# Attention's edge stage: scores spread by adding transposes instead of products with the identity

## The chip, the cores and the metric

The kernel runs on one core of a Trainium2 chip. The metric is the device time of one execution, in microseconds (us). It was run three times before the change: 25516.59, 25548.4 and 25451.02 us, median 25516.59.

## The reference, cut to what matters

Four graph layers follow one another on 6250 nodes and 206250 edges that are sorted by their destination. The change lies in the second, an attention layer. For each edge it makes four scores `a`, takes a softmax of them over the edges that share a destination, and sums weighted messages there:

```
a = (m1_s @ W_alpha).reshape(e, H, AS_)          # H = 4
a = jnp.where(a > 0, a, 0.2 * a)
a = jnp.sum(a * alpha_dot, axis=-1, keepdims=True)
amax = jax.ops.segment_max(a, dst, num_segments=n)
...
ex = jnp.exp(a - amax[dst])
den = jax.ops.segment_sum(ex, dst, num_segments=n)
alpha = ex / (den[dst] + 1e-16)
...
agg = jax.ops.segment_sum(alpha * h, dst, num_segments=n)
```

All values are 32-bit floats.

## The kernel before, in words

The program goes through its stages one after the other, each a block with five engine programs: prepare, sorting the edges (names `order_...`), the first layer's edges, its nodes, the attention layer's edges (`edge_layer1`), its nodes, and then edges and nodes twice more. Only `edge_layer1` is touched.

`edge_layer1` handles 1620 tiles of 128 edges, one edge on each partition. Each engine runs its own loop over steps; a turn of the loop is six steps, and there are six slots for what is loaded. In step s an engine works on several tiles of different age. TensorE (PE) in step s, from L1052 on:

- tile s-4 (`c`): the scores of the tile are spread into the PSUM tile `ps_x`. The product of L1060 first writes a mask (a large negative number where two edges have different destinations, 0 where they have the same) for four heads side by side, 512 columns. Then L1063 adds for each head h a 128x128 block in which every row holds the 128 scores of that head. Its stationary operand is the score column `crow[:, COMB + h]`, repeated 128 times by a stride of zero; its moving operand is the identity. VectorE (DVE) takes the maximum over the columns at L1262.
- tile s-1 (`n`): L1072 makes edge weights `ps_w`.
- tile s-2 (`a`): `turn` (L1041 to L1050) transposes the four blocks of `m1` into `ps_m1`, after a filling product (L1038) that writes what nobody reads.
- tile s-4: L1081 and L1083 make the heads' messages `ps_h`.
- tile s-3 (`b`): `turn` for `m2`.
- tile s-4: a filling product and L1095, which sums messages that share a destination into `ps_g`. It waits for DVE's `hw` (L1286), and DVE waits for it at L1298, at the end of DVE's step.
- tile s-2: L1102 and L1105 make `ps_a`, for which ScalarE (ACT) waits at L1132.

A product of 32-bit operands is two weight loads and two matmuls in the trace; a transpose of them (L1049) is one of each.

The running maximum and sums lie in DRAM, in six tables `comb0` to `comb5`, one for each slot, so tile t reads what tile t-6 wrote. GpSimd (POOL) moves them. In its step s it waits until the write of tile s-6 has landed (`written`, L1001), copies the indices of tile s (L1002), issues the gather of `srow` (L1007) and of `crow` (L1014) for tile s, and then the scatter of tile s-5 to its table (L1022), after waits on `kept` (ACT L1160) and `row_set` (DVE L1298) of that tile. SyncE (SP) loads `keys`, `rbf` and `yt` of a tile (L982, L985, L989) as soon as the slot is free; the first waits for `masks`, which DVE sets at L1292.

```
if t.reuses(SLOTS):
    ...
    pool.wait_ge(written[t.j], t.dma(1))
pool.tensor_copy(at[t.j][:, :], ...).then_inc(at_set, 1)
...
t = s.back(5)
...
pool.wait_ge(row_set, t.count(1))
pool.indirect_dma_start(out=combs[t.j], ...).then_inc(written[t.j], 16)
```

Of the kernel before, what the change touches and what calls it, by code (L numbers as in the profile page):

```python
# [113 lines left out]
def bcast(ap, shape):  # L114
    return ap.to_broadcast(list(shape))
# [805 lines left out]
def edge_layer1(nc, g, A, src_table, combs):  # L921
# [6 lines left out]
    with Phase(nc, "e1") as ph:  # L928
# [42 lines left out]
        with nc.Block() as block:  # L971
# [57 lines left out]
            def _(pe):  # L1029
# [6 lines left out]
                def fill(ps, columns):  # L1036

                    pe.matmul(ps[:, 0:columns].rearrange("p (k n) -> p k n", k=2), g.ident[:, :],  # L1038
                              bcast(g.ident[:, 0:columns // 2].unsqueeze(1), (P, 2, columns // 2)), start=True, stop=True)

                def turn(t, m, ps, ready, half, free, out, filled):  # L1041
                    if t.reuses(1):
                        pe.wait_ge(free, t.count(0))
                    if filled:
                        fill(ps, filled)
                    pe.wait_ge(ready, t.count(1))
                    pe.wait_ge(half, t.count(1))
                    for c in range(4):
                        ins = pe.transpose(ps[:, c * P:(c + 1) * P], m[t.j % 2][:, c * P:(c + 1) * P], g.ident[:, :])  # L1049
                    ins.then_inc(out, 1)  # L1050

                def step(s):  # L1052
                    a, b, c = s.back(2), s.back(3), s.back(4)
                    if c.exists():
                        k = c.j % 2
                        pe.wait_ge(lg_set, c.count(1))
                        if c.reuses(1):
                            pe.wait_ge(mx_set, c.count(0))

                        pe.matmul(ps_x[:, :].rearrange("p (h e) -> p h e", h=4), ident16[:, :],  # L1060
                                  bcast(apart[k][:, :].unsqueeze(1), (P, 4, P)), start=True, stop=False)
                        for h in range(4):
                            ins = pe.matmul(ps_x[:, h * P:(h + 1) * P], bcast(crow[c.j][:, COMB + h:COMB + h + 1], (P, P)), g.ident[:, :],  # L1063
                                            start=False, stop=h == 3)
                        ins.then_inc(x_ps, 1)
                    n = s.back(1)
                    if n.exists():
                        k = n.j % 2
                        pe.wait_ge(rbf_in[n.j], n.dma())
                        if n.reuses(2):  # L1070
                            pe.wait_ge(feats1, n.count(-1))
                        pe.matmul(ps_w[k][:, 0:224], rbf[n.j][:, :], WR[:, :], start=True, stop=True).then_inc(w_ps, 1)  # L1072
                    if a.exists():
                        turn(a, m1, ps_m1, feats1, sv1_set, m1T_set, m1_t, 192)
                    if c.exists():
                        k = c.j % 2
                        pe.wait_ge(m2T_set, c.count(1))
                        if c.reuses(1):
                            pe.wait_ge(hw_set, c.count(0))
                        heads = ps_h[:, 0:4 * (HD - 1)].rearrange("p (h m) -> p h m", h=4)  # L1080
                        pe.matmul(heads[:, :, 0:16], m2T[k][:, 0:P], WS2[:, :], start=True, stop=True)  # L1081
                        for q in range(3):
                            ins = pe.matmul(heads[:, :, 16 + 8 * q:24 + 8 * q], m2T[k][:, (q + 1) * P:(q + 2) * P], WV2[:, :],  # L1083
                                            start=True, stop=True)
                        ins.then_inc(h_ps, 1)
                    if b.exists():
                        turn(b, m2, ps_m2, feats2, sv2_set, m2T_set, m2_t, 0)
                    if c.exists():
                        k = c.j % 2
                        if c.reuses(1):  # L1090
                            pe.wait_ge(row_set, c.count(0))
                        fill(ps_g, 256)
                        pe.wait_ge(hw_set, c.count(1))
                        pe.wait_ge(den_set, c.count(1))
                        pe.matmul(ps_g[:, 0:4 * HD], same[k][:, :], hw[k][:, :], start=True, stop=True).then_inc(g_ps, 1)  # L1095
                    if a.exists():
                        k = a.j % 2
                        pe.wait_ge(m1T_set, a.count(1))
                        if a.reuses(1):
                            pe.wait_ge(ra_set, a.count(0))  # L1100
                            pe.wait_ge(vv_set, a.count(0))
                        pe.matmul(ps_a[:, 0:164], m1T[k][:, 0:P], WS1[:, :], start=True, stop=True)  # L1102
                        values = ps_a[:, 164:164 + 6 * CV].rearrange("p (r q m) -> p q r m", r=2, q=3)
                        for q in range(3):
                            ins = pe.matmul(values[:, q], m1T[k][:, (q + 1) * P:(q + 2) * P], bcast(WV1[:, :].unsqueeze(1), (P, 2, CV)),  # L1105
                                            start=True, stop=True)
                        ins.then_inc(a_ps, 1)
                run_steps(pe, step, 4, SLOTS, NT, COUNTS)

            @block.scalar  # L1110
# [922 lines left out]
```

## Time and profile before

| | us |
|---|---|
| median of 3 runs (25451.02 to 25548.4) | 25516.59 |
| span of the profiled execution, first to last instruction | 25427.1 |
| PE busy in the span | 19679.3 (77%) |
| DVE busy | 19154.8 (75%) |
| ACT busy | 12590.5 (50%) |
| POOL busy | 12879.8 (51%) |
| first and last instruction of L1063 | 6598.3 and 17441.3 |

For the profiled execution only the span is given, not a time of its own. The span is the time from its first to its last instruction; a run's time takes in what lies around that. "Busy" is the union of an engine's instructions. PE's matmuls are pipelined: the mean time of one (0.28 us) overlaps those of its neighbours, so what a matmul costs the engine is the distance from the start of one to the start of the next. The profile cuts the span into 40 slices; the attention layer's edges are slices 11 to 27.

### The profile page before, as it was taken

Reading aid. Unit: us, or ns where it says so; the run is one execution under the profiler, and the core shown is the slowest. Engines: PE = TensorE matmul, PEld = TensorE weight load, DVE = VectorE, ACT = ScalarE, POOL = GpSimd, SP = SyncE. Lnnn points to the kernel's source line nnn. Section 1 sums busy time; section 2 is a strip of 40 time slices with the busy share of each in tenths; the row PEclk is TensorE's granted clock in tenths of the full one; section 3 lists DMA queues with packets and bytes.
Section 4 is the critical chain, followed back from the end, with each engine's and each line's share of the span. In section 5 each row is a group of like instructions: output and inputs, shape, how many; then the busy total and the mean of one; then the engine's idle time right before and its main releaser. Section 6 shows DMA issues by size and latency. Waiting matters only on the chain. (4 is left out here: it accounts for less than half of the span.)

```text
span 25427.1 us, 480526 instructions
## 1 busy us (share of the span) xinstructions
PE 19679.3 (77%) x108650; PEld 15218.6 (60%) x108650; DVE 19154.8 (75%) x58214; ACT 12590.5 (50%) x42770; POOL 12879.8 (51%) x13907
## 2 busy tenths in 40 slices
PE   1466566565888889899989899985677799677799
PEld 1223222223677777778778777774555588555588
DVE  8333588887777778788878787878777688777688
ACT  0233344443577777777777777773333322333322
POOL 2777655664444444444444444442777500777500
PEclk6677788888999999999999999997999999999999
DMA  0466555555322222222222222223222200222200
GB/s 34 138 172 172 139 111 110 109 109 113 113 73 73 72 74 74 73 74 76 76 73 76 72 76 74 74 74 88 66 61 61 48 6 7 66 61 61 48 6 6
DMA packets 1776894, 1962.61 MB, mean 77 GB/s; under 512 B 754160, under 2 KB 1451744, under 8 KB 1776192
## 3 DMA queue, kind: packets, MB, share of 16 engines
q0 software_dynamic: 567456, 1314.26, 19.5%
q1 hardware_dynamic: 1209376, 647.65, 11.0%
q8 instruction: 24, 0.39, 0.0%
q14 instruction: 38, 0.31, 0.0%
HBM read 1399.54 MB, written 561.06 MB: 77 GB/s over the span
## 5 line engine op out<-in xcount | busy, mean ns | idle before, releaser
L1521 PE MATMUL e_sums<-e_feat,e_same 128*128 128x272 f32 x13824 | 3438.4, 403 | 1357.7 <-ACT e_feat L1542 1231.4
L1503 POOL DMA_INDIRECT e_rows<-x,e_take x3456 | 3609.3, 1044 | 1120.4 <-issue 1047.2
L1521 PEld LDWEIGHTS e_sums<-e_feat,e_same 128*128 128x128 f32 x13824 | 2593.6, 192 | 2202.1 <-issue 1590.7
L581 PE MATMUL e_sums<-e_feat,e_same 128*128 128x480 f32 x3456 | 1962.0, 724 | 1357.2 <-DVE e_feat L649 1357.2
L1049 PE MATMUL e_ps_m<-ident,e_m 128*128 128x128 f32 x12960 | 2092.9, 286 | 1073.6 <-ACT e_m L1122 1062.0
L565 POOL DMA_INDIRECT e_rows<-table,e_take x1728 | 1933.0, 1119 | 1347.0 <-issue 1300.8
L1116 ACT ACTIVATE e_m<-e_th,e_yt 128x64 f32<-128x64 f32 x6480 | 2324.4, 430 | 186.6 <-issue 9.4
L1049 PEld LDWEIGHTS e_ps_m<-ident,e_m 128*128 128x128 f32 x12960 | 1452.8, 145 | 1449.5 <-DVE e_m L1245 772.5
L581 PEld LDWEIGHTS e_sums<-e_feat,e_same 128*128 128x128 f32 x3456 | 803.0, 244 | 2516.8 <-issue 2411.3
L1007 POOL DMA_INDIRECT e_srow<-src_table,e_at x1620 | 1647.3, 1017 | 1248.9 <-POOL e_at L1002 952.5
L600 ACT ACTIVATE e_feat<-e_feat,e_pay 128x64 f32<-128x64 f32 x5184 | 1284.8, 334 | 1806.9 <-DVE e_feat L624 1717.1
L1539 ACT ACTIVATE e_feat<-e_rows 128x640 f32<-128x640 f32 x864 | 636.7, 737 | 3052.2 <-DMA e_rows<-x,e_take 2993.6
L1118 ACT ACTIVATE e_m<-e_qs,e_yt 128x64 f32<-128x64 f32 x6480 | 1723.1, 337 | 846.4 <-issue 816.1
L1002 POOL COPY e_at<-lists 128x3 int32 (+1 forms) x1620 | 354.2, 219 | 3355.0 <-DMA comb<-e_crow,e_at 3335.4
L1014 POOL DMA_INDIRECT e_crow<-comb,e_at x1620 | 1590.1, 982 | 571.8 <-issue 532.5
L1022 POOL DMA_INDIRECT comb<-e_crow,e_at x1620 | 1608.3, 993 | 510.3 <-issue 492.7
L322 POOL DMA_INDIRECT pay_rows<-order_stage,order_put x1620 | 1569.3, 969 | 493.7 <-issue 379.7
L709 POOL TENSOR_TENSOR n_stats<-n_stats,n_power 128x1 f32<-128x1 f32 x250 | 145.1, 580 | 3217.9 <-DVE n_stats L694 3130.7
L1063 PEld LDWEIGHTS e_ps_x<-ident,e_crow 128*128 128x128 f32 x12960 | 1719.4, 192 | 45.6
L1063 PE MATMUL e_ps_x<-ident,e_crow 128*128 128x128 f32 x12960 | 1716.2, 276 | 0.0
L363 PEld LDWEIGHTS order_ps_h<-order_feat,order_W 128*128 128x128 f32 x1620 | 344.7, 256 | 2047.1 <-DMA order_feat<-in_attr_T 1753.1
L363 PE MATMUL order_ps_h<-order_feat,order_W 128*128 128x128 f32 x1620 | 507.0, 407 | 1285.5 <-DMA order_feat<-in_attr_T 1282.7
(307 smaller groups left out, 53270.3 us busy)
## 6 DMA issues: line engine op xcount, KB each, us to landing
e_pay<-pay_rows SPq DMA_DIRECT2D x432, 470.0 KB, 3.9
order_keys<-key_row SPq DMA_DIRECT2D x810, 128.0 KB
e_keys<-key_row SPq DMA_DIRECT2D x1620, 64.0 KB, 3.0
e_rows<-x,e_take POOLq DMA_INDIRECT x3456, 2.6
order_feat<-in_attr_T SPq DMA_DIRECT2D x810, 64.0 KB, 3.6
comb<-n_comb SPq DMA_DIRECT2D x300, 164.0 KB, 1.9
e_rows<-table,e_take POOLq DMA_INDIRECT x1728, 4.0
pay_rows<-order_stage,order_put POOLq DMA_INDIRECT x1620
```

What stands on the lines that cost most here:

```text
L322: pool.indirect_dma_start(out=pay_rows, out_offset=bass.IndirectOffsetOnAxis(ap=put[t.j][:, q:q + 1], axis=0), in_=stage[t.j][:, q, :], in ...
L565: pool.indirect_dma_start(out=rows[t.j][:, q, 0:D], out_offset=None, in_=table, in_offset=bass.IndirectOffsetOnAxis(ap=take[t.j][:, q:q + ...
L581: ins = pe.matmul(sums[b][q // G][:, 0:AGG0], same[b][:, q, :], feat[b][:, q, 0:AGG0], start=q % G == 0, stop=q % G == G - 1)
L1007: pool.indirect_dma_start(out=srow[t.j][:, :], out_offset=None, in_=src_table, in_offset=bass.IndirectOffsetOnAxis(ap=at[t.j][:, 0:1], axi ...
L1014: pool.indirect_dma_start(out=crow[t.j][:, 0:COMB], out_offset=None, in_=combs[t.j][0:NP, :], in_offset=bass.IndirectOffsetOnAxis(ap=at[t. ...
L1022: pool.indirect_dma_start(out=combs[t.j], out_offset=bass.IndirectOffsetOnAxis(ap=at[t.j][:, 2:3], axis=0), in_=crow[t.j][:, 0:COMB], in_o ...
L1049: ins = pe.transpose(ps[:, c * P:(c + 1) * P], m[t.j % 2][:, c * P:(c + 1) * P], g.ident[:, :])
L1063: ins = pe.matmul(ps_x[:, h * P:(h + 1) * P], bcast(crow[c.j][:, COMB + h:COMB + h + 1], (P, P)), g.ident[:, :], start=False, stop=h == 3)
L1116: act.activation(to, v, ACT.Identity, scale=y(t, c), bias=y(t, c))
L1118: act.activation(to, v, ACT.Copy, scale=y(t, c))
L1503: pool.indirect_dma_start(out=rows[t.j][:, q, :], out_offset=None, in_=x, in_offset=bass.IndirectOffsetOnAxis(ap=take[t.j][:, q:q + 1], ax ...
L1521: ins = pe.matmul(sums[b][q // G][:, 512 * h:512 * h + HALF], same[b][:, q, :], feat[b][:, q, h * HALF:(h + 1) * HALF], start=q % G == 0, ...
```

## The change

The four products of L1063 and L1064 are issued with `is_transpose=True`. The operands, the output, the order and every wait are the same: the score column repeated 128 times is now transposed and added to the masks, where it was multiplied with the identity and added.

```
                         for h in range(4):
                             ins = pe.matmul(ps_x[:, h * P:(h + 1) * P], bcast(crow[c.j][:, COMB + h:COMB + h + 1], (P, P)), g.ident[:, :],
-                                            start=False, stop=h == 3)
+                                            is_transpose=True, start=False, stop=h == 3)
                         ins.then_inc(x_ps, 1)
```

## Rows read from the trace of the kernel before

**Rows 1.** The page: busy time of the engines; granted clock in 40 slices (tenths).

```profile
PE 19679.3 (77%) x108650; PEld 15218.6 (60%) x108650; DVE 19154.8 (75%) x58214; ACT 12590.5 (50%) x42770; POOL 12879.8 (51%) x13907
...
PEclk6677788888999999999999999997999999999999
```

**Rows 2.** Who waited for whom, 7000 to 17000 us: us, times, longest.

```profile
PE e_ps_m L1049 <- ACT e_m L1122: 980.0, 1900, 3.3
...
DVE e_crow L1298 <- PE e_ps_g L1095: 527.7, 1465, 1.5
...
DVE e_mv L1224 <- issue: 141.2, 126, 1.1
...
DVE e_mx L1262 <- PE e_ps_x L1063: 2.6, 8, 0.4
```

**Rows 3.** Groups of POOL, same stretch: xcount, busy us, mean ns, idle before, releaser.

```profile
L1007 POOL DMA_INDIRECT e_srow<-src_table,e_at x1490 | 1516.5, 1018 | 1148.6 <-POOL e_at L1002 876.1 <-DVE e_mv L1225 272.5
L1022 POOL DMA_INDIRECT comb<-e_crow,e_at x1489 | 1478.1, 993 | 453.7 <-issue 453.7
L1014 POOL DMA_INDIRECT e_crow<-comb,e_at x1489 | 1462.4, 982 | 527.1 <-issue 490.7 <-ACT e_crow L1160 33.7 <-DVE e_crow L1298 2.8
L1002 POOL COPY e_at<-lists 128x3 int32 x1490 | 326.3, 219 | 3088.3 <-DMA comb<-e_crow,e_at 3088.3
```

**Rows 4.** PE's timeline, one step: start us, us, line, count, idle before.

```profile
14000.84 0.60 PE L1049 MATMUL e_ps_m<-ident,e_m 128*128 128x128 f32 x4
...
14002.57 0.63 PE L1049 MATMUL e_ps_m<-ident,e_m 128*128 128x128 f32 x4 [0.31 <-ACT e_m L1122]
...
14003.47 0.44 PE L1095 MATMUL e_ps_g<-e_hw,e_same 128*128 128x164 f32 x2
...
14004.81 0.38 PE L1060 MATMUL e_ps_x<-e_apart,e_ident 128*128 128x512 bf16 x1
14005.02 1.05 PE L1063 MATMUL e_ps_x<-ident,e_crow 128*128 128x128 f32 x8
14006.00 0.64 PE L1072 MATMUL e_ps_w<-e_WR,e_rbf 16*128 16x224 f32 x2
```

**Rows 5.** Busy time, clock and DMA by stretches; the second lies in rows 6.

```profile
core 0: us, PE busy (x) PEld busy (x) DVE busy (x) ACT busy (x) POOL busy (x), PEclk, DMA share, GB/s
7000.00:17000.00 10000.00, 9006.82 (x61071) 7899.05 (x61070) 8010.39 (x34260) 7228.20 (x26811) 4783.15 (x5958) 0.96 0.26 74
...
11385.19:11388.02 2.83, 2.83 (x11) 2.65 (x11) 1.39 (x6) 1.31 (x5) 1.89 (x2) 0.50 0.41 101
```

**Rows 6.** PE's timeline in a stretch of low clock.

```profile
11385.19 1.09 PE L1049 MATMUL e_ps_m<-ident,e_m 128*128 128x128 f32 x4 [0.35 <-ACT e_m L1122]
11386.07 1.06 PE L1038 MATMUL e_ps_g<-ident 128*128 128x256 f32 x2
11386.93 0.76 PE L1095 MATMUL e_ps_g<-e_hw,e_same 128*128 128x164 f32 x2
```

**Rows 7.** Timeline of all engines: a scatter that lands promptly.

```profile
11354.00 0.32 DVE L1224 TENSOR_TENSOR e_mv<-e_srow,e_crow 128x160 f32<-128x160 f32 x1
...
11358.08 0.99 POOL L1022 DMA_INDIRECT comb<-e_crow,e_at  x1 [0.30 <-issue]
...
11359.55 0.33 SPq L982 DMA_DIRECT2D e_keys<-key_row  x1
...
11360.00 0.32 DVE L1224 TENSOR_TENSOR e_mv<-e_srow,e_crow 128x160 f32<-128x160 f32 x1
...
11360.84 0.18 POOL L1002 COPY e_at<-lists 128x3 int32 x1 [1.78 <-DMA comb<-e_crow,e_at]
```

**Rows 8.** The same: one that lands late.

```profile
11614.31 1.01 POOL L1022 DMA_INDIRECT comb<-e_crow,e_at  x1 [0.30 <-issue]
...
11614.63 0.33 SPq L982 DMA_DIRECT2D e_keys<-key_row  x1
...
11618.27 0.18 POOL L1002 COPY e_at<-lists 128x3 int32 x1 [2.96 <-DMA comb<-e_crow,e_at]
```

More of the change, by code:

```diff
@@ L1063, in step @@
                             ins = pe.matmul(ps_x[:, h * P:(h + 1) * P], bcast(crow[c.j][:, COMB + h:COMB + h + 1], (P, P)), g.ident[:, :],
-                                            start=False, stop=h == 3)
+                                            is_transpose=True, start=False, stop=h == 3)
                         ins.then_inc(x_ps, 1)
```

## The prediction

> **What bounds the kernel now.** The page comes first. PE and DVE are both busy for three quarters of the span, and no engine is near full [rows 1], so shares alone name no bound; the one stage that the change touches has to be read by itself. L1063 runs from 6598.3 to 17441.3 us: 10843 us for 1620 tiles, 6.69 us for each. In the undisturbed middle, 7000 to 17000 us, PE is busy for 90% of the time, DVE for 80%, ACT 72%, POOL 48% [rows 5]. That looks like a stage bound by PE. The waits and the groups by line say otherwise.
>
> POOL's groups [rows 3] can be added up to one step, each as busy time and idle time before it, divided by the 1490 tiles: L1002 0.22 us and 2.07 idle; L1007 1.02 and 0.77; L1014 0.98 and 0.35; L1022 0.99 and 0.30. The sum is 6.70 us, and the stage's step in that stretch is 10000 / 1490 = 6.71 us. So the reader is to see that POOL's loop accounts for the whole step, and what it waits for is not an engine's result: 2.07 us of it is the landing of the scatter that it has just issued, since the copy of tile t waits for the write of tile t-6, and that scatter is the last thing in POOL's step before. All that it is seen to wait for from ACT and DVE at L1014 is 33.7 + 2.8 us in 10000. The 272.5 us at L1007 that are put down to DVE are no wait for it: the idle time there is 0.77 us whomever it is put down to. At L1022, where it would wait for `row_set`, the end of the PE and DVE chain, there are 0.30 us each time and never more. POOL is 48% busy and sets the time: it is a loop of latencies.
>
> What would the others do if let? DVE's steps follow at 6.00 us where nothing holds it: L1224 starts at 11354.00 and 11360.00 [rows 7]. Every sixth step its loop turns, with 1.12 us before L1224 (141.2 us over 126 times) [rows 2], so 6.00 + 1.12/6 = 6.19 us. It has 0.5 us in hand against POOL's 6.70.
>
> PE waits 980.0 us for ACT's `m` before its transposes [rows 2], 0.66 us a step, although 90% busy.
>
> **The change, part by part.** It removes from each tile four of the eight matmuls of L1063 and four of its eight weight loads, and turns the other four of each into a transpose's. Nothing is moved, and no wait is added or dropped. No queue's order changes.
>
> The price on PE: the eight of L1063 take 1.05 us from the first start to the last end [rows 4]. The row nearest to the new ones is L1049, four transposes of the same size and type against the same identity: 0.60 and 0.63 us [rows 4]. So the change gives PE back 1.05 - 0.63 = 0.42 to 1.05 - 0.60 = 0.45 us a tile. Times 1620 that is 680 to 730 us of PE's time. What the rows before do not show is a transpose that adds to what lies in PSUM, and one whose transposed operand is one column repeated. The bounds: the four may be as dear as the eight (nothing gained), or as cheap as L1049. Dearer than eight would still have the 0.66 us a step of PE's waiting as cover. I take L1049's price.
>
> What of it lies on the path that sets the end: nothing that I can find. Directly behind L1063, DVE's L1262 waits 2.6 us in 10000 for `ps_x` [rows 2], so it gains nothing by having it earlier. Next on PE come L1072, the filling product and the transposes of `a`, then the heads, then those of `b`, which wait for ACT: the 0.45 us turn into a longer wait there (0.31 us now in the step at 14002.57 [rows 4]). L1095, for which DVE waits 527.7/1465 = 0.36 us a time [rows 2], comes behind that wait and so starts no earlier at the full clock. And were DVE earlier, POOL would still wait for its own scatter. The work that hides the edit is POOL's loop, 6.70 us; were that gone, DVE's 6.19 us would be next, and still not PE.
>
> The sum is therefore 0 of 25427.1 us, the span of the profiled execution. That span lies 89 us below the median and 24 us below the lowest of the three times, which hold what lies around it too. I put the forecast at the median less some 15 us: the last tiles of the stage have no new gathers and a few steps there may shorten. **25500 us.**
>
> **Second-order effects** carry the doubt. There are two.
>
> The clock. PE's granted clock is 0.96 of full in this stage [rows 5]; between its two levels, 2.4 and 1.2 GHz, that is 8% of the time at the lower, 870 us of the stage. It falls after PE has waited: in rows 6 PE waits 0.35 us for ACT, having waited longer in the same step before, and the stretch that follows is at 0.50 [rows 5]. There the path from the transposes of `b` to the end of L1095 takes 11385.19 to 11387.69, 2.50 us [rows 6], against 14002.57 to 14003.91, 1.34 us [rows 4]: 1.16 us that DVE sees. After the change PE waits 0.45 us a step more, so I expect more such stretches, perhaps half as many again, a granted clock of 0.93 to 0.96.
> The Trainium skill, "TensorE: Matmul & The Clock Gate", Part 4, says that a transpose doesn't count as PE being busy, so that the full clock doesn't engage for it; by that rule the change takes all eight matmuls of L1063 out of what keeps the clock up, and the sum would be that of the slower rival below. The trace so far speaks against its weight here: eight transposes already stand in each step, and the clock is 0.96.
>
> The landing. Of 1.78 us where it is prompt [rows 7], the scatter takes 2.96 us where it is late [rows 8]. The difference that I see is when SP issues `keys`: 1.47 us after the scatter's start in rows 7, 0.32 us after it in rows 8. `keys` follows DVE's L1292, so DVE's phase against POOL decides it. The mean, 2.07 us, is (2.07 - 1.78)/(2.96 - 1.78), a quarter of the steps late. The change can move that phase through the clock alone: a DVE that is made late after a stretch of low clock issues `keys` well behind the scatter.
>
> **The rivals.**
> - *Faster by phase.* More stretches of low clock keep DVE behind POOL, and late landings become rare. All prompt: 0.29 x 1620 = 470 us off, 25040; half of it, 25270. For it: DVE has the 0.5 us in hand. Against: nothing aims at it.
> - *Slower by phase.* The other way: half the steps late in place of a quarter, 25980.
> - *PE is the bound after all.* Then the whole 0.42 to 0.45 us shows, 24790 to 24840. For it: 90% busy, and DVE waits for L1095 in nearly each step. Against: the sum of rows 3.
> - *Slower by clock.* PE falls to 1.2 GHz in each step at the wrong place. DVE's step becomes 6.19 + 1.16 = 7.35 us and DVE becomes the bound: 0.65 x 1620 = 1050 us more, 26570. It decides once (6.70 - 6.19)/1.16 = 44% of the steps are hit. Now it can be no more than 870/2.50 = 350 steps, 21%. For it: the longer wait on PE. Against: it takes twice as many.
> - *The change doesn't do what it says.* The adding transposes cost what the products cost, and the time stays, 25520.
>
> **How the numbers follow.** A measurement of this kernel can tell about 0.5% from no change, 128 us. Forecast 0.48, the edit without effect 0.05: within 0.5% together 0.53. Faster by phase 0.22 and PE as the bound 0.05: faster 0.27. Slower by clock 0.12 and by phase 0.08: slower 0.20. The range takes in two thirds of the phase's gain, down to 25200 (25516 less 315), and half its loss and the lower part of the clock's, up to 25740. Left out are the case of a bound PE, the full clock case and the ends of the phase cases, together some 0.2. The unknown price of the adding transpose lies wholly within, as it is hidden at either bound.
>
> **What would show each step.** L1063 as 6480 matmuls in place of 12960, four in 0.6 us; PE's busy share in the stage down by 6 to 7 points; the wait of L1049 for ACT up by about 0.45 us a step, or some 600 us; POOL's sum again equal to the step, with L1022's idle at 0.30; L1002's idle near 2.07 us; the clock a little below 0.96; the stage 10,800 us long. I am wrong if L1002's idle moves by over 0.08 us (that times 1620 is 0.5%), if L1022 begins to wait for DVE, or if the stage shortens while POOL's idle stays.

## The result

| | before | after |
|---|---|---|
| median, us | 25483.81 (4 runs) | 25167.04 (4 runs) |
| lowest to highest, us | 25420.36 to 25548.4 | 25097.93 to 25280.0 |
| span of the profiled execution, us | 25427.1 | 25278.4 |

The changed kernel is faster by 1.1%: the ratio is 0.9886, with a 95% interval of 0.9861 to 0.9911. The forecast was 25500 and the range 25200 to 25740, so the measured time lies 33 us below the range. It lies where the rival "faster by phase" had its times, 25040 to 25270, which had been given a chance of 0.22. The profiled execution is the slowest of the four (25280.0 us), so the profile below shows about half of what the median gained.

The page of the changed kernel, busy times and granted clock, beside [rows 1]:

```profile
PE 19552.8 (77%) x102170; PEld 14695.3 (58%) x102170; DVE 19105.4 (76%) x58214; ACT 12546.8 (50%) x42770; POOL 12879.8 (51%) x13907
...
PEclk6677788887899998999999999996999999999999
```

The stretch from 7000 to 17000 us, in the columns of [rows 5]: PE, PEld, DVE, ACT and POOL busy, then clock, DMA share and GB/s.

```profile
7000.00:17000.00 10000.00, 9019.31 (x56078) 7533.27 (x56076) 8107.15 (x34859) 7314.69 (x27280) 4835.31 (x6061) 0.92 0.27 75
```

PE issues 56078 matmuls in 10000 us in place of 61071, and is still busy for 90%. The granted clock has gone from 0.96 to 0.92. That tells what became of most of the 0.45 us a tile. They are not idle time: PE's idle time is 0.67 us a tile before and 0.65 after, and its busy time only falls from 6.04 to 5.95 us. At 0.96 PE is at 1.2 GHz for 8% of the time, at 0.92 for 16%, and at that clock the same work takes longer: L1049's four transposes take 1.09 us [rows 6] where they take 0.60 [rows 4].

The waits in that stretch (us, times, longest), beside [rows 2]:

```profile
POOL e_at L1002 <- DMA comb<-e_crow,e_at: 2767.8, 1515, 3.2
...
PE e_ps_m L1049 <- ACT e_m L1122: 931.3, 2346, 1.3
...
DVE e_crow L1298 <- PE e_ps_g L1095: 749.6, 1508, 1.5
...
DVE e_mv L1224 <- issue: 283.6, 253, 1.1
...
POOL comb L1022 <- DVE e_crow L1298: 245.5, 127, 3.6
```

PE's wait for ACT has not grown with the change: 931.3 us where it was 980.0. DVE's wait for L1095 has, from 527.7/1465 = 0.36 us to 749.6/1508 = 0.50 us a time. And a wait that didn't exist has appeared, POOL's for DVE before the scatter, 245.5 us. One wait is gone from the list. It is this one of the kernel before, DVE's for the gather that POOL had issued:

```profile
DVE e_mv L1224 <- DMA e_crow<-comb,e_at: 582.2, 675, 3.5
```

In the kernel before DVE was often at POOL's heels, waiting for the gather of its tile. The changed kernel's list of waits doesn't have this one at all: there DVE runs behind.

POOL's groups (busy, mean ns, idle before), beside [rows 3]:

```profile
L1022 POOL DMA_INDIRECT comb<-e_crow,e_at x1515 | 1525.7, 1007 | 691.5 <-issue 446.1 <-DVE e_crow L1298 245.5
L1007 POOL DMA_INDIRECT e_srow<-src_table,e_at x1516 | 1521.9, 1004 | 1168.6 <-POOL e_at L1002 1073.6 <-DVE e_mv L1225 95.1
L1014 POOL DMA_INDIRECT e_crow<-comb,e_at x1515 | 1463.9, 966 | 537.4 <-issue 456.8 <-DVE e_crow L1298 78.8 <-ACT e_crow L1160 1.8
L1002 POOL COPY e_at<-lists 128x3 int32 x1515 | 323.8, 214 | 2767.8 <-DMA comb<-e_crow,e_at 2767.8
```

Per tile: L1002 0.21 us and 1.83 idle, L1007 1.00 and 0.77, L1014 0.97 and 0.35, L1022 1.01 and 0.46. The sum is 6.60 us, and the step is 10000 / 1515 = 6.60 us; it was 6.70 and 6.71. That the two agree says nothing by itself, since the busy and idle time of any engine add up to its step. What says something is who ended the idle time. Two terms have moved: the wait for the scatter's landing is down by 0.24 us, and the wait before the scatter is up by 0.16, which is DVE's (245.5/1515). The smaller terms move by 0.02 us or less each. The step is 0.11 us shorter, and that times 1620 is 178 us. POOL's landing is still its largest wait, but DVE is now close behind it (see "The scatter issued first"). The stage, from the first to the last L1063, is now 10678 us, 165 less than before (the three numbers after x6480 are the shortest, median and longest matmul in ns):

```profile
L1063 PE MATMUL e_ps_x<-ident,e_crow x6480: 270/273/421, 6609.3 to 17287.6; 128*128 128x128 f32 x197
```

The timeline shows why the landing is prompt:

```profile
11350.19 0.33 SPq L982 DMA_DIRECT2D e_keys<-key_row  x1
...
11352.96 0.60 PE L1063 MATMUL e_ps_x<-ident,e_crow 128*128 128x128 f32 x4
...
11353.89 1.21 POOL L1022 DMA_INDIRECT comb<-e_crow,e_at  x1 [0.30 <-issue]
...
11356.89 0.21 POOL L1002 COPY e_at<-lists 128x3 int32 x1 [1.78 <-DMA comb<-e_crow,e_at]
...
11358.48 0.33 SPq L982 DMA_DIRECT2D e_keys<-key_row  x1
```

The last load of `keys` before the scatter of 11353.89 was issued 3.70 us ahead of it, the next one comes 4.59 us after its start, and POOL's copy follows after 1.78 us of idle time. In [rows 7] `keys` came 1.47 us after the scatter, in [rows 8] 0.32 us after, with 2.96 us of idle time.

Over all scatters of the kernel before (the first and last 25 tiles left out, and 9 scatters that had `keys` 2.0 to 1.0 us ahead), sorted by when SP issued the last `keys` that began within 3 us after the scatter's start or ahead of it, the mean time from the scatter's start to POOL's next copy is:

| keys after the scatter's start, us | scatters | us to the copy |
|---|---|---|
| before -4.0 | 36 | 2.78 |
| -4.0 to -2.0 | 70 | 2.79 |
| -1.0 to -0.5 | 11 | 3.62 |
| -0.5 to 0 | 77 | 3.59 |
| 0 to 0.5 | 267 | 3.85 |
| 0.5 to 1.0 | 209 | 3.14 |
| 1.0 to 1.5 | 571 | 2.78 |
| 1.5 to 3.0 | 320 | 2.79 |

One timeline is one scatter, so the same sort was done for the changed kernel's trace. In the kernel before, 564 of 1570 scatters had `keys` within 1 us of their start; in the changed kernel 28 of 1570 have. Most of them, 897, have it 4.0 to 2.0 us ahead, and these take 2.80 us to the copy. The mean over all scatters falls from 3.06 to 2.83 us, which is the 0.24 us by which the idle time of L1002 fell.

The wait that low clock brings shows in the trace too. All 127 waits of POOL for DVE before the scatter follow a stretch with PE at 1.2 GHz: from 9 to 1 us ahead of the scatter the granted clock is 0.70 on average. The longest come where a whole step of DVE lies in such a stretch. That step takes 9.69 us where an undisturbed one takes 6.00, and POOL waits 3.6 us. This stretch (columns as above) and its scatter are one of 28:

```profile
7454.67:7464.36 9.69, 9.69 (x38) 8.35 (x38) 5.44 (x24) 4.70 (x18) 3.83 (x5) 0.50 0.25 78
```

```profile
7465.53 0.99 POOL L1022 DMA_INDIRECT comb<-e_crow,e_at  x1 [3.61 <-DVE e_crow L1298]
```

### The profile page after: what moved, and what is told of

It is laid out like the page before. It is cut to its first block and busy times, and to the rows that moved or that the text cites. A ratio compares the mean times of both kernels' runs of the same rounds, so it can differ in the third digit from the quotient of the medians.

```text
span 25278.4 us, 467566 instructions
## 1 busy us (share of the span) xinstructions
PE 19552.8 (77%) x102170; PEld 14695.3 (58%) x102170; DVE 19105.4 (76%) x58214; ACT 12546.8 (50%) x42770; POOL 12879.8 (51%) x13907
## 5 line engine op out<-in xcount | busy, mean ns | idle before, releaser
L1049 PE MATMUL e_ps_m<-ident,e_m 128*128 128x128 f32 x12960 | 2238.4, 300 | 1050.4 <-ACT e_m L1122 1001.3
L1049 PEld LDWEIGHTS e_ps_m<-ident,e_m 128*128 128x128 f32 x12960 | 1512.2, 152 | 1591.5 <-DVE e_m L1245 883.3
L1007 POOL DMA_INDIRECT e_srow<-src_table,e_at x1620 | 1626.1, 1004 | 1248.9 <-POOL e_at L1002 1147.6
L1022 POOL DMA_INDIRECT comb<-e_crow,e_at x1620 | 1631.1, 1007 | 759.4 <-issue 474.5
L1002 POOL COPY e_at<-lists 128x3 int32 (+1 forms) x1620 | 346.7, 214 | 2971.3 <-DMA comb<-e_crow,e_at 2952.1
L1014 POOL DMA_INDIRECT e_crow<-comb,e_at x1620 | 1565.3, 966 | 572.5 <-issue 489.2
L1132 ACT ACTIVATE e_th<-e_ps_a 128x96 f32<-128x96 f32 x1620 | 405.3, 250 | 2098.7 <-PE e_ps_a L1105 2090.5
L1105 PEld LDWEIGHTS e_ps_a<-e_WV,e_m1T 128*128 128x128 f32 x9720 | 1423.4, 212 | 0.0
```

Source lines behind the costliest of these rows:

```text
L1007: pool.indirect_dma_start(out=srow[t.j][:, :], out_offset=None, in_=src_table, in_offset=bass.IndirectOffsetOnAxis(ap=at[t.j][:, 0:1], axi ...
L1014: pool.indirect_dma_start(out=crow[t.j][:, 0:COMB], out_offset=None, in_=combs[t.j][0:NP, :], in_offset=bass.IndirectOffsetOnAxis(ap=at[t. ...
L1022: pool.indirect_dma_start(out=combs[t.j], out_offset=bass.IndirectOffsetOnAxis(ap=at[t.j][:, 2:3], axis=0), in_=crow[t.j][:, 0:COMB], in_o ...
```

## The experiments

Two theories stood. **Phase:** POOL's loop is the bound, and the 64 KB load of `keys`, 128 partitions of 512 bytes, holds the scatter up where it is issued close to it. PE's lighter work lets the clock fall more often, that makes DVE late, and a late DVE issues `keys` at a harmless time. **PE:** part of the saved 0.45 us lay on a path that the waits don't show. Below, "idle" is POOL's idle time before its copy for each tile, and the step is the stretch divided by its tiles. Where a line was added, the numbers of the lines behind it are one or two higher than in the kernel before.

### Filling products back in

```
                         if c.reuses(1):
                             pe.wait_ge(mx_set, c.count(0))
+                        fill(ps_x, 256)
```

> The changed kernel with a filling product of 256 columns put ahead of the mask product in ps_x, two matmuls that take about the 0.43 us that the transposes gave back; nobody reads what it writes. Both theories expect the time of before, 25,480 within 0.5%: by the phase theory with L1002's idle back at 2.0 to 2.1 us and the clock back at 0.96; by a theory in which the transposes themselves hold the clock down (they would not count as work), the clock stays near 0.92 to 0.93 and the time near 25,170.

Measured: 25472.5 us, ratio 1.001 (0.9989 to 1.0031) to the kernel before. The gain is gone. The stretch from 7000 to 17000 us, and POOL's copy:

```profile
7000.00:17000.00 10000.00, 9046.88 (x58220) 7581.25 (x58219) 8023.06 (x34332) 7245.32 (x26868) 4787.79 (x5971) 0.96 0.26 74
```

```profile
L1002 POOL COPY e_at<-lists 128x3 int32 x1492 | 321.5, 215 | 3077.6 <-DMA comb<-e_crow,e_at 3077.6
```

Clock 0.96, idle 3077.6/1492 = 2.06 us, as in the kernel before. So the gain needs PE's shorter time and not the transposes. Nor do the transposes, twelve a tile here in place of eight, hold the clock down. What this run can't tell apart is PE's shorter time and the low clock that comes with it; the trace with the scatter moved does, further down.

### A filling product out, with the products kept

```
-                        turn(a, m1, ps_m1, feats1, sv1_set, m1T_set, m1_t, 192)
+                        turn(a, m1, ps_m1, feats1, sv1_set, m1T_set, m1_t, 0)
```

> The kernel before (products, not transposes) without the filling product of 192 columns ahead of the transposes of m1, which nobody reads: PE gets back 0.32 us a tile ahead of a wait for ACT, without a transpose being involved. Phase theory: low-clock stretches grow, the clock falls to 0.93 to 0.95, DVE falls behind, L1002's idle falls towards 1.85 us, and the time falls by 150 to 320 us, to 25,160 to 25,330. PE theory: the same direction, but with L1002's idle unchanged at 2.07. If the effect is one of the transposes alone: no change.

Measured: 25113.1 us, ratio 0.9865 (0.9839 to 0.9892). Without a single new transpose the gain is there. It lies 47 us below the range that was expected, and its interval overlaps that of the change under study.

```profile
7000.00:17000.00 10000.00, 8783.70 (x59964) 7808.09 (x59962) 8216.25 (x35361) 7435.65 (x27672) 4929.30 (x6148) 0.94 0.27 76
```

```profile
L1002 POOL COPY e_at<-lists 128x3 int32 x1537 | 310.7, 202 | 2873.6 <-DMA comb<-e_crow,e_at 2873.6
```

Clock 0.94, idle 2873.6/1537 = 1.87 us, step 6.51 us. This is the changed kernel's pattern: more low clock, prompter landings. Only 132 of 1570 scatters have `keys` within 1 us of their start. "PE theory" expected an unchanged 2.07, and falls: the 0.20 us by which the idle time fell, times 1620, are 324 us, and the kernel is 329 us faster than the one before in the same batch of runs (25441.7).

### The keys load moved, PE left alone

```
                     if t.reuses(SLOTS):
                         sp.wait_ge(masks, t.count(1 - SLOTS))
+                        sp.wait_ge(feats1, t.count(3 - SLOTS))
                     sp.dma_start(keys[t.j][:, :], ...)
```

> The kernel before, with one more wait on SP: the load of keys for a tile waits also for feats1 of a tile two younger, which DVE sets some 2.9 us later than masks. PE's work is the products of before. Phase theory (the scatter lands late when the keys load is issued close behind it): landings become prompt, L1002's idle time falls from 2.07 to about 1.8 us, POOL's step from 6.70 to 6.45, and the time falls by 300 to 450 us to 25,050 to 25,200, with the granted clock of before or above it. PE theory (part of the 0.45 us that PE got back lay on the path): PE's work is unchanged, so the time stays at 25,480 within 0.5%.

Measured: 25280.65 us, ratio 0.9932 (0.9908 to 0.9957). The direction is that of the phase theory; the size is half.

```profile
L1003 POOL COPY e_at<-lists 128x3 int32 x1516 | 298.5, 197 | 3013.1 <-DMA comb<-e_crow,e_at 3013.1
```

Idle is 3013.1/1516 = 1.99 us where 1.8 was expected. Sorted as in the table above, 1234 of the scatters had `keys` 2.0 to 1.5 us before them, with 2.89 us to the copy, but 258 had it 1.5 to 0 us before, with 3.35 to 3.60. The load had been moved nearly round to the next scatter. SP issues its loads in one order, so a wait ahead of `keys` can also hold back `rbf` and `yt` behind it; the run that makes `keys` small, below, leaves these alone. So the wait was set anew for 1.9 us, with `prods` in place of `feats1`:

```
+                        sp.wait_ge(prods, t.count(3 - SLOTS))
```

> The kernel before, with SP's load of keys waiting also for prods of a tile two younger: 1.9 us later than masks, where the wait for feats1 was 2.9 us. The loads of keys in the first runs landed around the scatters as follows: late where keys was issued from 1.5 us before to 0.8 us after the scatter's start, prompt elsewhere; the wait for feats1 put a fifth of them into that stretch from the other side. Phase theory: with 1.9 us keys comes 3.1 us after one scatter and 3.2 us before the next, L1002's idle falls to 1.8 us, POOL's step to 6.42 us, the time to 25,000 to 25,080. If late landings have another cause, 25,250 as with feats1, or above.

Measured: 25052.23 us, ratio 0.9857 (0.9832 to 0.9882), as forecast.

```profile
7000.00:17000.00 10000.00, 9180.32 (x63443) 8057.64 (x63443) 8305.96 (x35596) 7510.76 (x27856) 4983.85 (x6190) 0.98 0.27 77
```

```profile
L1003 POOL COPY e_at<-lists 128x3 int32 x1547 | 346.5, 224 | 2804.1 <-DMA comb<-e_crow,e_at 2804.1
```

Idle is 2804.1/1547 = 1.81 us, the step 6.46 us, and the clock has risen, to 0.98. PE's wait for ACT is shorter too, 803.8 us in place of 980.0, so late landings had probably kept PE waiting; that was not tried by itself.

### The same wait in the changed kernel

> The changed kernel with the same added wait on SP. In the changed kernel keys is issued some 4 us after the scatter, so 2.9 us more brings it round to the next scatter, a step of 6.5 us on. Phase theory: late landings come back, L1002's idle above 1.95 us, and the time is at or above that of the changed kernel, 25,170 to 25,450; if the phase finds another place of its own, no change. PE theory: no change, 25,170. A theory in which the wait is good by itself: as much faster as in the kernel before.

Measured: 25068.56 us, ratio 0.9849 (0.9824 to 0.9873) to the kernel before; the changed kernel's 0.9886 (0.9861 to 0.9911) overlaps it.

```profile
L1003 POOL COPY e_at<-lists 128x3 int32 x1532 | 335.0, 219 | 2905.7 <-DMA comb<-e_crow,e_at 2905.7
```

Idle is 2905.7/1532 = 1.90 us, up from 1.83: some late landings came back, as expected, but fewer than thought (above 1.95 had been expected), and the time, expected at 25,170 or above, did not rise. In this run POOL waits for DVE no more than 10.3 us before its gather and never at the scatter, where the changed kernel lost 245.5. From 7000 to 16000 us the changed kernel has 42 steps of DVE that lie wholly at 1.2 GHz and take 9.69 us; this run has 3. Why the low clock falls otherwise here was not tried, and "the wait is good by itself" is not excluded. As a test of the theories it is inconclusive.

### The keys load made small

The load now fills one partition. The lines shown are those of the step; ahead of it DVE sets the six `keys` tiles to 0 once, and SP waits for that. The mask is multiplied by 0, so this kernel leaves out the masking and its output is not that of the reference.

```
-                    sp.dma_start(keys[t.j][:, :], g.key_row[...].partition_broadcast(P)).then_inc(keys_in[t.j], 16)
+                    sp.dma_start(keys[t.j][0:1, :], g.key_row[...].partition_broadcast(1)).then_inc(keys_in[t.j], 16)
...
-                        dve.tensor_scalar(apart[kb][:, :], keys[b.j][:, :], key, LOW, ALU.not_equal, ALU.mult).then_inc(masks, 1)
+                        dve.tensor_scalar(apart[kb][:, :], keys[b.j][:, :], key, 0.0, ALU.not_equal, ALU.mult).then_inc(masks, 1)
```

> The kernel before with the keys load cut to one partition (512 bytes in place of 64 KB), issued when it was before. Left out: the comparison of keys (the masks are those of blank tiles and are multiplied by 0), so the output is not the reference's; every instruction's size on the engines is kept. Phase theory: with the load gone nothing collides with the scatter, whatever the phase: L1002's idle 1.78 us, the time 25,000 to 25,080. If it is the loads of rbf and yt, or the scatter's own descriptors, that are late: unchanged, 2.07 us and 25,440.

Measured: 25022.66 us, ratio 0.9842 (0.9817 to 0.9868).

```profile
L1003 POOL COPY e_at<-lists 128x3 int32 x1553 | 336.3, 217 | 2790.5 <-DMA comb<-e_crow,e_at 2790.5
```

Idle is 2790.5/1553 = 1.80 us. With the load issued at the same point and 127 of its 128 partitions gone, the late landings are gone: 184 scatters still have `keys` within 1 us of their start, but with `keys` 0 to 0.5 us after the start the copy now comes after 2.97 us where it was 3.85, and with 0.5 to 1.0 us after 2.84 where it was 3.14. It is the `keys` load that they come from. Moving it (25052) gets nearly all that removing it does (25023).

### DVE made late by itself

A memset that nobody reads, behind L1298, first of 128 columns and then of 256:

```
+                        dve.memset(extra[:, :], 0.0)
```

> The kernel before with one instruction more in each of DVE's steps, a memset of 128x128 that nobody reads, behind L1298; PE and POOL as they were. DVE's own step grows by some 0.1 to 0.2 us, to 6.3 to 6.4 us. Phase theory: a DVE that can no longer catch up with POOL stays clear of the phase in which keys falls on the scatter, so work added to an engine that does not bound makes the kernel faster: L1002's idle below 1.95 us and the time 25,050 to 25,300. Any theory in which PE's saved time or the clock acts directly: no change or slower, 25,430 to 25,600.

Measured: 25435.07 us, ratio 1.0012 (0.9995 to 1.0028): a miss. The memset is busy for 165 ns, but DVE's undisturbed step grew by only 0.07 us, from 6.00 to 6.07. The rest seems to fit into waits that were there; which, was not traced. The memset's row, 7000 to 16000 us:

```profile
L1300 DVE MEMSET e_extra<- 128x128 f32 x1356 | 223.7, 165 | 0.0
```

With the loop's turn DVE's step was 6.27 us, still below POOL's 6.4 with prompt landings. The profiled execution is the fastest of the twelve (25328.61 us). The dose was raised:

> The memset behind L1298 is 128x256 in place of 128x128. The smaller one lengthened DVE's undisturbed step by only 0.07 us, 6.00 to 6.07 and with the loop's turn 6.27, still shorter than POOL's step of 6.38 us with prompt landings, so that DVE went on catching up. The larger one should add some 0.2 us: 6.40, just longer than POOL's. Phase theory: now DVE stays behind, L1002's idle falls to 1.8 to 1.9 us, and the time to 25,050 to 25,250, PE's work and its filling products as in the kernel before. Any other theory: no change or slower by up to 0.2 x 1620 = 320 us, 25,440 to 25,760.

Measured: 25058.25 us, ratio 0.9874 (0.9855 to 0.9893).

```profile
L1300 DVE MEMSET e_extra<- 128x256 f32 x1388 | 377.5, 272 | 3.8
```

```profile
L1003 POOL COPY e_at<-lists 128x3 int32 x1543 | 317.7, 206 | 2841.9 <-DMA comb<-e_crow,e_at 2841.9
```

```profile
DVE e_mv L1225 <- DMA e_crow<-comb,e_at: 52.6, 64, 2.6
```

The only edit is 272 ns of useless work on DVE in each step, 377.5 us of it in the 9000 us from 7000 to 16000 (the first row; the others are for 7000 to 17000), and the kernel is 1.3% faster. DVE's undisturbed step is 6.20 us, and 6.40 with the loop's turn. Idle is 2841.9/1543 = 1.84 us, DVE's wait for the gather is down to 52.6 us from 582.2, and 86 of 1570 scatters have `keys` within 1 us of their start in place of 564. So DVE's lag alone is enough. It needs no fall of the clock, which is 0.98 here:

```profile
7000.00:17000.00 10000.00, 9192.53 (x63312) 7958.64 (x63310) 8566.02 (x37059) 7505.51 (x27796) 4950.39 (x6173) 0.98 0.27 77
```

### The scatter issued first

POOL's block for tile s-5 is moved from the end of its step to the beginning, ahead of the wait for `written`:

```
                 def step(s):
+                    t = s.back(5)
+                    if t.exists():
+                        ...
+                        pool.wait_ge(row_set, t.count(1))
+                        pool.indirect_dma_start(out=combs[t.j], ...).then_inc(written[t.j], 16)
                     t = s
```

> The kernel before with POOL's scatter of tile s-5 moved ahead of the copy and gathers of tile s, so that its landing is hidden behind the two gathers and POOL no longer waits for what it has just issued. POOL's loop as the bound: POOL's step without the wait is 4.9 us, DVE's 6.19 us becomes the bound, and the time falls by up to 0.45 x 1620 = 730 us, to 24,720 to 24,850; L1002's idle near 0, L1022 waits for DVE. If POOL were not the bound: little change.

> The changed kernel with the same scatter moved. PE theory (the 0.45 us lie on a path that POOL hid in part): faster than the kernel before with the scatter moved, by up to 700 us. Phase theory: nothing on PE's path is shortened that DVE waits for at the full clock, while each stretch of low clock now shows in full, so it is no faster than that one and up to 300 us slower: 24,750 to 25,100.

Measured: 24739.09 us with the products, ratio 0.9734 (0.9709 to 0.9759), and 25200.48 us with the transposes, 0.9916 (0.9889 to 0.9942). With POOL's loop opened, the change under study costs 461 us. That is the direction that the phase theory expected, but more than the 300 us it allowed. And opening the loop gains the changed kernel nothing: 25200 against 25167 us, 0.9916 against 0.9886 of the kernel before. First the rows with the products (7000 to 16000 us, then waits), then those with the transposes:

```profile
7000.00:16000.00 9000.00, 8296.46 (x58986) 7391.11 (x58985) 7699.01 (x33088) 6999.62 (x25895) 4502.76 (x5755) 1.00 0.28 79
```

```profile
POOL comb L1001 <- DVE e_crow L1298: 2833.1, 1394, 4.1
...
DVE e_crow L1298 <- PE e_ps_g L1095: 358.5, 1438, 1.4
```

```profile
7000.00:16000.00 9000.00, 8067.21 (x50832) 6737.03 (x50831) 7356.05 (x31592) 6634.63 (x24724) 4298.99 (x5494) 0.93 0.26 76
```

```profile
POOL comb L1001 <- DVE e_crow L1298: 3108.3, 1331, 5.5
...
DVE e_crow L1298 <- PE e_ps_g L1095: 653.9, 1374, 1.5
```

POOL now waits for DVE in nearly each step. The step is 9000/1439 = 6.25 us with the products and 9000/1374 = 6.55 with the transposes; 0.30 us times 1620 is 486 us, near the difference of the two times, 461. The clock is 1.00 against 0.93, and DVE's wait for L1095 0.25 us against 0.48 (358.5/1438 and 653.9/1374). That is 0.23 of the 0.30.

Is it the low clock, or the transposes themselves? Sorted by the granted clock in them, DVE's steps in these two traces tell. Those that lie wholly at the full clock take 6.31 us with the transposes (850 steps) and 6.24 with the products (1394). The steps with low clock in them take 6.95 us with the transposes, and there are 523 of them where the products have 43. At the full clock the change costs DVE next to nothing; the loss lies in the other steps.

This also says what limits the changed kernel with the scatter in its place. POOL's step with prompt landings is 6.70 - 0.29 = 6.41 us. DVE's own step is 6.25 us with the products, so it catches up with POOL; with the transposes it is 6.55, so it doesn't.

Then the filling product of 256 columns was added to the second, and one of 128 columns to the first:

> The changed kernel with the scatter moved, and the filling product of 256 columns ahead of the mask product, so that PE works as long as with the products. If the 460 us by which the transposes lose with the scatter moved are the clock's, given up by PE's idle time: back to 24,740 within 100 us, granted clock back to 0.98. If they are the transposes' own (they do not count as work, or the adding transpose is late for somebody): it stays near 25,200 and 0.93 to 0.95.

> The kernel before with the scatter moved and a filling product of 128 columns added, 0.21 us more of PE's time in each step, ahead of the mask product. With the scatter moved the time hangs on DVE's step of 6.19 us and on what low clock adds to it. If the clock still costs there: its stretches become rarer, 24,650 to 24,720. If PE is then too full (it had 0.49 us a step of waiting for ACT): as much slower.

Measured: 24730.17 us, ratio 0.9727 (0.9708 to 0.9745), and 24728.74 us, ratio 0.9729 (0.971 to 0.9748). The first with its rows:

```profile
7000.00:16000.00 9000.00, 8344.83 (x56086) 7070.67 (x56087) 7705.95 (x33076) 6995.85 (x25889) 4502.64 (x5753) 1.00 0.27 79
```

```profile
POOL comb L1001 <- DVE e_crow L1299: 2830.5, 1393, 4.1
...
DVE e_crow L1299 <- PE e_ps_g L1096: 350.5, 1438, 1.4
```

Clock 1.00 and 0.24 us for L1095: all 460 us come back with two matmuls a tile that nobody reads, which make PE as busy as it is with the products (5.80 us a step, 5.77 there). Together with the steps sorted by clock this puts the loss down to the clock. One more of them in the kernel with the products changed nothing (24728.74 us, where 24,650 to 24,720 had been expected if the clock still cost); it was 1.00 already. These three, at 24729 to 24739 us, are the fastest versions of the study, some 1.6% ahead of the changed kernel.

## Why the prediction was wrong

- **POOL's loop as the bound** held for the kernel before: opening the loop gave 2.7% where up to 730 us (2.9%) had been put on it before the run. The argument in the prediction was weaker than it looks. A sum of POOL's busy and idle time equals the step whoever sets it; the part that carries is that nearly none of the idle time was ended by another engine's result. For the changed kernel it held only in part: opening the loop there gave nothing.
- **The price on PE** held: 6480 matmuls, four in 0.60 us, 0.45 us a tile.
- **"What of it lies on the path: nothing"** held for PE's path. With PE's time left as it was and only `keys` moved the kernel is at 0.9857, and with PE's shorter time and the loop opened it is slower, not faster.
- **"The 0.45 us turn into a longer wait" for ACT** failed. The wait of L1049 was to grow by some 600 us and PE's share to fall by 6 to 7 points; neither moved (980.0 to 931.3 us, 90% and 90%). Most of the time went into low clock, whose share doubled from 8% to 16%. The forecast had said half as many stretches again and 0.93 to 0.96; it is 0.92.
- **The weight of the phase is the step that failed:** the sum put the change of the scatter's landing at 0, L1002's idle "near 2.07 us". It measured 1.83, 0.24 us a step or 390 us of the stage, of which DVE's lateness took back 0.16 us a step. The text had the mechanism, its price of 0.29 x 1620 = 470 us, and the link from the clock to DVE's lag to `keys`, and then took it for a second-order effect of either sign. It was the first-order effect, and of one sign: DVE's 6.19 us against POOL's 6.4 with prompt landings leaves 0.2 us a step, not the 0.5 us that I counted against the mean of 6.70. A doubled share of low clock uses that up, as the 0.2 us of the second memset did: with the loop opened DVE's step is 6.55 us with the transposes and 6.25 with the products. The rival's "half of it, 25270, all of it, 25040" holds the measured 25167.
- **The wait of L1022 for DVE** was named as a sign of being wrong. It came, 245.5 us, each of the 127 waits behind a stretch of low clock.
- **The rule of the Trainium skill** ("TensorE: Matmul & The Clock Gate", Part 4), that a transpose doesn't count as PE being busy, is not borne out for the 32-bit transposes of this kernel. With as much PE time in either, twelve transposes a tile and eight have the same clock, 0.96 with the scatter in its place and 1.00 with it moved. And taking out products with no transpose in their place lowers it too, to 0.94.

Still open: the profiled execution shows 149 us of the 317 by which the medians differ, so the two terms of POOL's sum are shown in kind, but not for the whole gain. The profiled execution has a granted clock of 0.892 over its span and the three faster ones 0.897 to 0.898, which fits a smaller loss to low clock in them; their stages were not seen. Open too is why the same wait on SP made the changed kernel no slower.

## What to carry to other kernels

Where an engine that is half idle sets the time by a loop of latencies, add up its own groups first, and look at who ended each idle time, since the sum alone comes out for every engine; then ask which other transfers are issued near the one that it waits for, since work taken from an engine off the path can shift them. Here the edit was worth 1% by such a shift; moving the transfer gave 1.4% and opening the loop 2.7%, and with the loop open the same edit was a loss of 1.9%. Before crediting a saving on TensorE, put the same time back as filling products: if the gain goes and the clock returns, it was PE's time and clock, and not the operation.

## What the runs showed of the hardware

- A load of 64 KB to 128 partitions, issued by SP from 1 us before to 1 us after the start of an indirect scatter of POOL (128 rows), delays its landing by 0.4 to 1.1 us (POOL's next copy comes after 3.14 to 3.85 us in place of 2.78, the table above). Issued 1.5 to 1.0 us before the start it still cost 0.6 us in the run with the wait for `feats1` (3.35 us, 47 scatters). Issued 1.0 us or more after the start it costs nothing (2.78). With one partition in place of 128 the delay is nearly gone (2.84 to 2.99 us).
- A transpose of 32-bit floats adds to what a product has left in PSUM, at the price of one that doesn't: 0.60 us for four. Four products of the same shape take 1.05 us.
- Useless work on VectorE, 272 ns a step, made the kernel faster by 1.3% (0.9874, 0.9855 to 0.9893).
- A whole step of VectorE took 9.69 us with PE at 1.2 GHz and 6.00 undisturbed (the changed kernel, 7454.67 us).
